# Expert blocks of a routed feed-forward layer: the second layer three steps behind the turned rows, eight weight buffers, and other places for the loading of finished groups

## The reference

```
x = x + norm(linear_attention(norm(x)))                  # 16 heads of 8, causal sums over each sequence
x = x + norm(shared(norm(x)) + routed(norm(x)))

shared = new_gelu(xf @ Wfc_s + bfc_s) @ Wproj_s + bproj_s        # 128 -> 512 -> 128
probs  = softmax(xf @ Wr);  topk_p, topk_i = top_k(probs, 2)     # 8 experts, 2 for each token
routed = sum over the 2 experts e of a token:
         (new_gelu(xf @ Wfc[e] + bfc[e]) @ Wproj[e] + bproj[e]) * gate
```

## Time and profile before

| what | before |
|---|---|
| median of 3 runs | 405.58 us (405.35 to 405.91) |
| the profiled execution, its own time | 401.68 us |
| its span, first to last instruction | 399.9 us |
| TensorE busy | 344.3 us (86%) |
| VectorE busy | 293.0 us (73%) |
| ScalarE busy | 258.2 us (65%) |
| GpSimd busy | 267.0 us (67%) |
| mean granted TensorE clock | 0.954 of full |

### The profile page before, as it was taken

The page is one execution under the profiler, slowest core; times in us unless marked ns, Lnnn a source line. Parts: engine busy times, 40 slices in busy tenths (PEclk is TensorE's granted clock), DMA queues, the critical chain, the costliest instruction groups (busy, mean ns, idle before and its releaser), DMA issues.

```text
span 399.9 us, 8165 instructions
## 1 busy us (share of the span) xinstructions
PE 344.3 (86%) x2523; PEld 299.6 (75%) x2523; DVE 293.0 (73%) x685; ACT 258.2 (65%) x692; POOL 267.0 (67%) x335
## 2 busy tenths in 40 slices
PE   6867799999797997979887977599998999998883
PEld 3436378687776877757686966499998999998863
DVE  4998699999999996999934432376453547867656
ACT  4978557887777957667244634355555576678664
POOL 7788696579787895787676637556565455577640
PEclk9999989999999996999999669599999999999998
DMA  6588369382735125052039326299887779988317
GB/s 197 161 230 218 68 185 161 105 219 67 228 102 161 59 84 154 21 145 73 21 95 373 96 76 207 77 274 276 267 244 233 224 253 375 298 267 252 124 36 211
DMA packets 53521, 69.17 MB, mean 173 GB/s; under 512 B 6365, under 2 KB 37386, under 8 KB 53482
## 3 DMA queue, kind: packets, MB, share of 16 engines
q1 hardware_dynamic: 47556, 58.58, 51.1%
q0 software_dynamic: 4544, 9.35, 6.7%
q10 hardware_dynamic: 1382, 0.79, 0.7%
HBM read 40.06 MB, written 18.15 MB: 146 GB/s over the span
## 4 chain that ended last, share of the span: by engine, by line
PE 31%; DVE 12%; issue 7%; another core or an unknown queue 4%; DMA 2%; POOL 1%; ACT 1%; SPq 0%; POOLq 0%; DVEq 0%; ACTq 0%
PE bO L1523 8%; PE bS L1523 7%; DVE KV L1673 2%; PE bV L1496 2%; PE bV L1498 2%; PE bV L1497 2%; DVE SH L2024 1%; DVE KV L1664 1%; DVE w_lo L2075 1%; PE bA L1496 1%; PE bB L1498 1%; PE bB L1497 1%; PE bB L1496 1%; PE bT L1358 1%
## 5 line engine op out<-in xcount | busy, mean ns | idle before, releaser
L814 POOL DMA_INDIRECT expert_results<-yb,yrow x78 | 79.4, 1018 | 60.9 <-DVE yb L2107 37.2
L691 POOL DMA_INDIRECT expert_lists<-rows,pos x64 | 64.7, 1010 | 19.2 <-issue 19.2
L1673 DVE TENSOR_TENSOR_SCAN KV<-bS,KV 128x1024 f32<-128x1024 bf16 x32 | 72.8, 2279 | 0.6 <-POOL KV L715 0.3
L1314 PEld LDWEIGHTS bO<-wout_rot,Z 128*128 128x128 f32 x512 | 63.0, 198 | 10.8 <-POOL Z L771 3.8
L1314 PE MATMUL bO<-wout_rot,Z 128*128 128x128 f32 x512 | 65.7, 284 | 5.3 <-POOL Z L724 2.7
L2099 DVE COPY yrow<-xb 128x2 int32<-128x2 int32 x24 | 4.3, 178 | 44.7 <-PE bO L1523 21.0
L1133 ACT ACTIVATE hs<-bV,KV 128x256 f32<-128x256 f32 x56 | 21.9, 476 | 17.0 <-PE bV L1498 13.3
L1523 PE MATMUL bO<-KV,hs 128*128 128x128 f32 x232 | 30.6, 287 | 0.0
L1523 PEld LDWEIGHTS bO<-KV,hs 128*128 128x128 f32 x232 | 29.2, 203 | 0.1
L1284 PE MATMUL bA<-w2s_sb,hs 128*128 128x128 f32 x224 | 28.8, 277 | 0.0
L1496 PE MATMUL bV<-x_lo,w_hi 128*128 128x256 f32 x80 | 24.4, 305 | 3.6 <-DVE x_lo L2078 3.1
(11 more groups left out here) (369 smaller groups left out, 1003.6 us busy)
## 6 DMA issues: line engine op xcount, KB each, us to landing
KV<-packed_weights SPq DMA_DIRECT2D x21, 578.0 KB
Z<-packed_weights SPq DMA_DIRECT2D x18, 578.0 KB
xb<-expert_lists SPq DMA_DIRECT2D x39, 129.0 KB
vr<-vr SPq DMA_DIRECT2D x16, 224.0 KB
shared<-expert_results SPq DMA_DIRECT2D x7, 512.0 KB, 5.2
vr<-vr SPq DMA_DIRECT2D x16, 192.0 KB
vr<-vr SPq DMA_DIRECT2D x16, 160.0 KB
vr<-vr SPq DMA_DIRECT2D x16, 128.0 KB
```

The lines of the kernel that those rows point to most:

```text
L691: g.indirect_dma_start(out=lists, out_offset=bass.IndirectOffsetOnAxis(ap=pos[:, m:m + 1], axis=0), in_=rows[:, m // TILES, m % TILES, :], ...
L814: g.indirect_dma_start(out=results, out_offset=bass.IndirectOffsetOnAxis(ap=yrow[n][:, c], axis=0), in_=yb[n][:, c, :], in_offset=None).th ...
L1314: ins = t.matmul(bO[:, j * D:(j + 1) * D], Z[:, d, j * P:(j + 1) * P], wout_rot[:, d], start=False, stop=True, skip_group_check=True)
L1673: v.tensor_tensor_scan(w, ps_keep, w, 0.0, ALU.mult, ALU.add).then_inc(s["kv_sum"], 1)
```

## The change

It moves steps of the expert blocks against each other, gives two kinds of data more buffers, and moves entries of four tables.

- **TensorE.** From step 5 on, step b holds F(b-1), T(b+1), S(b-3): rows are turned a step earlier, the second layer comes a step later (`HELD = 3`, `SHIFT = 5`, `finished(b)`). The hardware loop is gone; all steps are written out.
- **Buffers.** Eight weight buffers instead of six (`NW = 8`); the two new ones lie in `vr`, which the attention part leaves free. A third place for the gelu's output, `third`. Weights of block b now wait for `blk_yr >= b - 7`. Rows of a block are loaded ahead of its weights and have a wait of their own, for the rows of block b-4 to have been split (`blk_tr`), from block 30 on for the gelu of block b-6.
- **VectorE.** `yrow(b-1)` is copied right behind `x_lo(b)`; `yb(b-3)` follows at the end of step b. The work of the final part moves with it, one step later.
- **SyncE.** The results of groups 0 to 3 are loaded behind blocks 28, 29, 30, 32 instead of 26, 27, 28, 30, those of group 4 behind 35 instead of 34.

Semaphores that were used for one thing each are merged (`root_steps`, `fin_act`, `link`) to make room for those of the new buffers.

```diff
     NBUF = 6
+    NW = 8
+    HELD = 3
+    SHIFT = 5
...
-    Y_AFTER = {26: 0, 27: 1, 28: 2, 30: 3, 34: 4, 38: 5}
+    Y_AFTER = {28: 0, 29: 1, 30: 2, 32: 3, 35: 4, 38: 5}
...
-        wb = [kvz[n // 3][:, (n % 3) * WROW:(n % 3 + 1) * WROW] for n in range(NBUF)]
+        wb = [kvz[n // 3][:, (n % 3) * WROW:(n % 3 + 1) * WROW] for n in range(6)]
+        in_vr = vr[:].rearrange("p e t -> p (e t)")[:, 2 * STEP:2 * STEP + 2 * WROW]
+        wb += [in_vr[:, n * WROW:(n + 1) * WROW] for n in range(2)]
...
+        def finished(b):
+
+            if b <= SHIFT:
+                return b - 2 if 2 <= b < SHIFT else None
+            return b - HELD
...
-                if from_on(b, NBUF):
-                    sp.wait_ge(s["blk_yr"], b - NBUF + 1)
+                if b >= NW:
+                    sp.wait_ge(s["blk_yr"], b - NW + 1)
                     alone(sp)
+                if b == 6:
+                    sp.wait_ge(s["kv_sum"], 4 * NS)
...
+                if b >= NBUF and b - NBUF < SHARED_FROM:
+                    sp.wait_ge(s["blk_tr"], b - NBUF + 3)
+                    alone(sp)
+                elif b >= NBUF:
+                    sp.wait_ge(s["blk_gelu"], b - NBUF + 1)
+                    alone(sp)
...
+                if b > 1:
+                    load_rows(b, n)
                 load_weights(b, n)
-                if not isinstance(b, int) or b > 1:
-                    load_rows(b, n)
...
-            ROOTS_AFTER = {28: 0, 32: 1}
+            ROOTS_AFTER = {27: 0, 31: 1}
...
-                if not isinstance(b, int) or 1 < b < NB:
-                    rows_turned(b, n, turn)
-                if from_on(b, 1) and (not isinstance(b, int) or b - 1 < NB):
-                    first_layer(b, n, turn)
+                if 2 < b <= SHIFT:
+                    rows_turned(b)
+                if 1 <= b <= NB:
+                    first_layer(b - 1)
+                if SHIFT <= b < NB - 1:
+                    rows_turned(b + 1)
...
-                if from_on(b, 2):
-                    second_layer(b, n)
-                if at == 8:
+                if b == 9:
                     table_turned(1, s["blk_yr"], 6)
-
-            over_blocks(pe, step, extra=2, first=2)
+                if finished(b) is not None:
+                    second_layer(finished(b))
+
+            each_block(step, extra=HELD)
...
-            GATED_AT = {25: 0, 27: 1, 29: 2, 31: 3, 33: 4, 37: 5}
-            MOMENTS_AT = {26: 0, 28: 1, 30: 2, 32: 3, 34: 4, 38: 5}
+            GATED_AT = {26: 0, 28: 1, 30: 2, 32: 3, 34: 4, 38: 5}
+            MOMENTS_AT = {27: 0, 29: 1, 31: 2, 33: 3, 35: 4, 39: 5}
```

More of the change, by code:

```diff
@@ L233, in sandwich_kernel @@
         x_lo = [sb(f"x_lo{n}", [P, BLK], F32R) for n in range(2)]
-        hb = [hs[:].rearrange("p c (n t) -> p n c t", n=2)[:, n] for n in range(2)]
+        third = sb("third", [P, CH, BLK])
+        hb = [hs[:].rearrange("p c (n t) -> p n c t", n=2)[:, n] for n in range(2)] + [third[:]]
         yb = [sb(f"yb{n}", [P, 2, D]) for n in range(NBUF)]
@@ L310, in alone, with weights_in @@
             eng.sem_inc(s["waited"], 1)
[L312 to L324 removed]
+        def weights_in(eng, b):
+            eng.wait_ge(wb_in[b % NW], 16 * (b // NW) + 16)
+        def finished(b):
+            if b <= SHIFT:
+                return b - 2 if 2 <= b < SHIFT else None
+            return b - HELD
         def each_block(step, extra=0):
@@ L2074, in step @@
                 if not isinstance(b, int) or b < NB:
[L2075 removed]
+                    v.tensor_tensor(w_lo[n % 2][:], wb[b % NW][:, 0:HID], w_hi[n % 2][:].bitcast(F32), ALU.subtract
                                     ).then_inc(s["blk_wlo"], 1)
```

196 lines of the change are left out of this document (92 added, 104 removed).

## The result

The changed kernel is not faster. Beside the kernel before on one chip, 13 runs each, its time is 1.009 times that of before (95% interval 1.0056 to 1.0125): some 3.7 us slower, where 1.5 us faster was forecast. Timed again beside before on two other chips, the changed kernel came to 1.0105 (1.005 to 1.0161) and 1.0016 (0.9966 to 1.0066). By these ratios it is slower on two chips of three. By the medians of all runs (407.53 against 407.02, 382.16 against 378.99, 403.61 against 403.93 us) it is clearly slower on one, the second. So the gain that was forecast did not come on any chip; how large the loss is stays unsharp.

The account below looks back on a forecast made before the run. TensorE was taken as the bound of the blocks' quiet middle, only its idle gaps fillable; 0.7 - 0.6 - 0.3 + 1.5 + 0.4 - 0.2 = +1.5 us, so 405.58 became 404.1 us, range 401.0 to 407.3 (8 in 10).

Parts of the forecast that it names:

- the tail: End behind the last F: last scatter earlier by 0.9 us beyond F(38)'s 1.5; +0.4 us taken, bounds -1.0 and +0.9.
- F(38): Step 38: gated of group 5 moves behind x_lo(38), so F(38)'s 1.52 us wait goes; +1.5 us, bounds 0 and 1.5.
- The cancelling rival: Whole kernel: gains and losses cancel, late signals fall elsewhere, F(38)'s 1.52 us not there to win; 405.5 us, chance 0.26.
- S one step later: Middle blocks: S's waits for the gelu shrink, 0.95 us of waiting left at F(19); +0.7 us, bounds 0 and 1.8.
- Low parts: VectorE under the final part: 0.14 us less slack at four waits, -0.6 us; step 35 overfull by moments, -0.3 us.
- The start: First expert blocks: VectorE no longer waits for S(3), but one S less is done before F(6); -0.2 us, bounds -1.8 and +1.6.
- Loads: Group results, rows and weights: nothing waits anew although the loads' places move; cost 0.
- a rival with 3.4 us: Blocks: a load or fetch is late, one or two waits of 1.3 to 3.4 us; about 407.5 us, chance 0.07.
- The loop: TensorE's written-out steps: 18 more block bodies to fetch, neither gain nor cost; 0.
- VectorE becomes the bound, slower: Steps 26 to 36 and the end: late signals and delayed yb cost 2.1 us; 407.7 us, chance 0.17.
- the signs named for a right forecast: Steps 12 to 38: no S wait for hs, F(38) unwaiting; last scatter 2.7 to 4 us behind S(38), earlier in absolute time.

Follow-up runs that it names:

- t_early: The changed kernel with the second layer back at two steps behind (S(b-2)), rows still turned a step early; 0.9948 of the kernel before, on a quiet chip.
- the three t_early: On late chips: t_early timed twice more (0.9908; median 403.75 against 403.93 us, no ratio), and once with rows turned early only from step 12 (0.9929).
- start_as_before: The changed kernel with SHIFT = 12 instead of 5, so the start keeps the order of the kernel before; 1.0117 of the kernel before, six runs.
- after_third: The changed kernel itself, unedited, timed again beside the kernel before on a late chip; 1.0016 of the kernel before.
- s_late_again: s_late_only timed again on another late chip; 0.9872 of the kernel before, six runs.
- loop_out: The kernel before with only TensorE's hardware loop written out; 1.008 (0.9999 to 1.016) of the kernel before.
- s_late_only: The changed kernel with T(b) back ahead of F(b-1), so only the second layer is late; 0.9896 of the kernel before, seven runs, late chip.
- tail_as_before: The changed kernel with the second layers of steps 37 to 40 placed as in the kernel before; 1.0052 (0.9992 to 1.0111) of the kernel before.
- f38_alone: The kernel before with gated of group 5 at step 38 instead of 37, moments at 39 instead of 38; 0.9994 of the kernel before, quiet chip.
- after_again: The changed kernel itself, unedited, timed again beside the kernel before on a quiet chip; 1.0105 of the kernel before.
- paced_start: The kernel before with six more GpSimd waits for TensorE's signals among the start's scatters; 1.0032 of the kernel before, quiet chip.

## Why the prediction was wrong

**The step that failed is the tail**, +0.4 us, and with it the +1.5 us of F(38). The text says of three second layers behind the last F: "its first half can be scattered from about 377.0, and three blocks take until 384.5". It counted blocks 36 to 38 from F(38) on and left out block 35. Before, block 35 was read out three microseconds ahead of F(38) (374.38 against 377.53); with S a step later it stands behind it, and two scatters more, 2.5 us, lie in GpSimd's queue. The forecast was that the time from F(38) to the end gets 0.4 us shorter. Measured, it got longer: from 22.4 to 26.9 us in the pair of traces, from 23.0 to 26.0 as the means of five and five traces on late chips, from 21.8 (three) to 23.5 (one) on quiet ones. The low bound, -1.0, was too near as well. `yb(35)` comes 46.0 to 48.4 us behind F(25) with S 2 and 49.5 to 50.9 with S 3 on late chips, 41.2 to 42.4 and 46.4 on quiet ones. From `yb(35)` to the last scatter are 11.3 to 14.4 us and from there to the end 11.6 to 13.4, with either order.

For the whole piece from F(25) to the end the terms gave +1.5 + 0.4 - 0.6 - 0.3 = +1.0 us. It went from 73.3 us (mean of five) to 75.3 (mean of five) on late chips, from 66.6 (three) to 69.6 (one) on quiet ones: -2.0 and -3.0 us.

How strong this is differs by chip. On quiet chips the chain of work that ended last runs through GpSimd's last scatters back to back in all four traces of the table, and t_early against the changed kernel, one edit on one chip, gives 3.4 us in the trace and about 1.5% in time. There it is shown that the second layer's lateness, through the scatters behind `yb(35)`, lengthens the end. On late chips that chain runs through the scatters back to back only in start_as_before, after_third and s_late_again; in before, loop_out and s_late_only it comes to the last scatters by way of the second layers of the last blocks, and in the changed kernel's own trace, in tail_as_before and in the three t_early it runs through ScalarE's wait for a late signal of TensorE (8.6, 4.2 and 3.6 us). There both limits are near each other, and which of them the later second layer moves is not separated.

**F(38), +1.5.** The wait went, as said: the piece F(25) to F(38) shrank from 50.2 and 51.6 to 48.7 to 49.6, and the gain was given back behind it. But the term took one execution for the rule. The text held that `gated` ahead of F(38) is in every execution; it is, and yet of the seven traces with the tables of before only one has a wait at F(38). The cancelling rival had named just this, that "the 1.52 us of F(38) aren't there to be won".

**S one step later, +0.7.** The waits of S for `hs` went, but F waited for `x_lo` 2.16 us where 0.95 was forecast: -0.7 in this trace. On a quiet chip none of these waits exists in either order: F(9) to F(38) holds no wait of S for `hs` in f38_alone. There was nothing to win there; after_again has two waits of F for `x_lo` instead, 0.63 and 0.49 us, where f38_alone has none.

**Low parts, -0.6 and -0.3.** Thirteen periods of 3.42 us are 44.5 of the 50.2 us before; without F(38)'s 1.52 there remain 4.2, and 5.1 of the 49.6 now. That is -0.9, the size forecast, but for this pair of traces: the other kernels with S 3 on late chips keep 4.2 to 5.1, and loop_out, which had no wait at F(38), kept 7.1. The agreement is luck as much as sense. Step 35 shows 0.75 us (372.28) where 0.3 was forecast.

**The start, -0.2.** F(0) to F(9) took 1.8 us longer in this trace, the lower bound, but 52.5 in after_third: the spread of one program is larger than the term. On a quiet chip the new order starts faster (34.3 against 35.8) and then loses more to the rows of block 11.

**Loads, 0.** Wrong on a quiet chip: T(11) waited 2.76 us for its rows. The text named this as a rival with 3.4 us and gave it 0.07. In the traces of late chips it doesn't show, since TensorE is late itself there.

**The loop, 0.** No idle time in its place between 262 and 330 us in loop_out's trace; its time is not settled (above).

The rival nearest to what came was "VectorE becomes the bound, slower", 407.7 us: right in sign and in one of its places (the end), wrong in its engine; its 2.1 us stand against some 3.7 by the ratio and 0.5 by the medians of all runs. The 1.0 us that it put there hung on a delayed `yb(36)`; what lengthened the end on quiet chips is GpSimd's queue behind `yb(35)`. Of the signs named for a right forecast, the last scatter was to end 2.7 to 4 us behind S(38); it ended 5.5 us behind it (392.35 against 386.82), and later in absolute time.

**What stays open.** The whole times don't add up from the end alone: by the ratios s_late_only and t_early are both faster than before by about 1%, both moves together are not; by the medians of all runs the gains are 0.0 to 1.0%. It would fit that the rest of the change (buffers, rows loaded ahead of weights, tables) wins more than the early turn or the late S costs, and that the two together eat it up; the rest without either move wasn't tried. The best kernel of this study is t_early: 0.9948 (0.9898 to 0.9997) and 0.9908 (0.9866 to 0.995), on one chip of each kind; in the third comparison its gain didn't show in the medians. In which stretch it wins, its traces don't show.

## What to carry to other kernels

When a stage is moved back to give its producer slack, follow its output to the very end: in the middle a step of delay may be free, but behind the last block it is paid once, by the queue that drains the results (here eight scatters of 1.26 us; 2 to 3 us of a step of 3.4 were paid). Find out which instruction the end hangs on (in several traces: here it was not the same one in all), measure from it to the end in both kernels, and doubt a gain at any instruction that it doesn't hang on. And take more than one trace on more than one chip before a gap is priced: here the first blocks take 54.7 us (mean of ten traces) on some chips and 35.4 (four) on others, and the wait of 1.52 us that the largest term was built on stands in one trace of seven.

## What the runs showed of the hardware

**Chips differ by 7% on one program.** The kernel before took 375.6 and 379.0 us (medians) on two chips and 403.8 to 407.0 on four others. Most of it is in the start: 34 to 38 us from F(0) to F(9) against 52 to 59. On quiet chips TensorE's signals arrive within 0.01 us of the recorded end. On late chips they arrive up to 12.4 us late there (that of F(4) in s_late_only), in batches. In the changed kernel's trace VectorE waited 11.19 us and got signals of four operations at once, 2.3 us behind the end of twelve scatters without a pause (239.26 to 254.11):

```profile
256.42 0.42 DVE L1885 CAST x_hi<-bT 128x256 fp32r<-128x256 f32 x1 [11.19 <-remote]
```

On late chips the batches came about 1 to 2.3 us behind the end of a run of scatters, at the start and at the end of the blocks. In the middle the same stands behind four scatters in a row: those from 297.05 to 301.81 in the trace before, with the late gelu of the earlier trace rows at 302.79, and those from 288.18 to 292.93 in the changed kernel's, with a gelu at 293.92. That is a coincidence in time, seen often; paced_start, the one run that was to break up the scatters in the start, fell on a quiet chip. On quiet chips 43 scatters in a row held nothing. What a late chip has is not shown. One mark of it is that records are lost there: of the 16 completions of a load of rows between 228 and 252 us the late traces hold 0 to 7, the quiet ones 14 to 16.

The Trainium skill, NOTIFIC — the notification-queue block, section Overflow: three behaviours, one of which stalls the engine, says that the block which writes such records pushes back on its producers when its inner queues fill, and that this can throttle an engine. Late signals would fit that. The lost records would not by themselves: the page puts losses at a full ring, another of the three behaviours, and not at the inner queues. No run here shows either. Every run on record has a span and a granted clock beside its time, so none is known to have gone without such records, and whether a late chip is as slow without them stays open.
